# Causal mask of the maxima moved to VectorE, weight parts to GpSimd, and two score units of each half merged

## What is computed

```python
H, D = (NUM_HEADS, HEAD_DIM)                       # 32 heads of 16
qkv = hidden_states @ w_attn + b_attn
scores = jnp.einsum('bqhd,bkhd->bhqk', q, k) * SCALE
bias = slopes[:, None, None] * rel[None, :, :]     # rel = key position - query position
causal = rel <= 0
scores = jnp.where(causal[None, None], scores + bias[None], -jnp.inf)
attn = jax.nn.softmax(scores, axis=-1)
out = jnp.einsum('bhqk,bkhd->bqhd', attn, v).reshape(B, S, HIDDEN)
return out @ w_proj + b_proj
```

## Time and profile before

| what | us |
| --- | --- |
| median of 3 runs (1851.12 to 2012.93) | 1870.08 |
| the profiled execution | 1866.97 |
| its span, first to last instruction | 1865.1 |
| busy in the span: PE / DVE / ACT / POOL | 1744.0 / 1366.6 / 987.7 / 119.7 |

### The profile page before, as it was taken

One profiled execution on the slowest core, in us unless ns is written; L12 is line 12 of the kernel. 1 busy time (PEld: TensorE's weight loads), 2 busy tenths in 40 slices (PEclk: granted clock), 3 DMA queues, 4 the chain that ended last, 5 costly groups with the idle time before them and its releaser, 6 DMA issues. The chain is left out here.

```text
span 1865.1 us, 35240 instructions
## 1 busy us (share of the span) xinstructions
PE 1744.0 (94%) x14412; PEld 904.9 (49%) x14412; DVE 1366.6 (73%) x2495; ACT 987.7 (53%) x1169; POOL 119.7 (6%) x218
## 2 busy tenths in 40 slices
PE   6997999999999999999799998899999999999697
PEld 4553433333333333333347677555555555543486
DVE  3765799999999999996464542588787878762485
ACT  3332277777777777778301111056666666655210
POOL 3323000000000000000010000100000000002000
PEclk9998799999999999999899999999999999975699
DMA  7768304332333333321524246815445444511221
GB/s 212 211 190 213 63 15 87 65 70 53 53 53 56 53 53 53 64 46 58 149 64 135 69 115 208 160 28 107 81 80 89 72 84 77 87 30 56 83 85 68
DMA packets 116865, 167.67 MB, mean 90 GB/s; under 512 B 20828, under 2 KB 58092, under 8 KB 116588
## 3 DMA queue, kind: packets, MB, share of 16 engines
q1 hardware_dynamic: 114880, 160.11, 38.1%
q0 software_dynamic: 1824, 5.31, 1.6%
HBM read 100.34 MB, written 64.50 MB: 88 GB/s over the span
## 5 line engine op out<-in xcount | busy, mean ns | idle before, releaser
L513 DVE TENSOR_REDUCE a_mxp<-a_ps_m 128x1 f32<-128x512 f32 x1024 | 634.2, 683 | 48.3 <-PE a_ps_m L377 44.9
L492 ACT ACTIVATE a_p<-a_ps_s 128x1024 f32<-128x1024 f32 x512 | 522.4, 1025 | 170.6 <-PE a_ps_s L417 160.9
L513 DVE TENSOR_REDUCE b_mxp<-b_ps_m 128x1 f32<-128x512 f32 (+3 forms) x768 | 382.3, 551 | 116.8 <-PE b_ps_m L377 109.6
L492 ACT ACTIVATE b_p<-b_ps_s 128x1024 f32<-128x1024 f32 (+3 forms) x384 | 308.8, 810 | 231.3 <-PE b_ps_s L417 229.0
L377 PE MATMUL a_ps_m<-a_slot_qk 48*128 48x512 f32 x640 | 240.0, 452 | 0.9
L417 PE MATMUL a_ps_s<-a_slot_qk 50*128 50x512 f32 x640 | 233.1, 445 | 1.2
L436 PE MATMUL a_ps_o<-a_p,a_slot_v 128*32 128x256 f32 x2560 | 205.6, 390 | 10.0 <-ACT a_p L492 5.4
L417 PEld LDWEIGHTS a_ps_s<-a_slot_qk 50*128 50x128 f32 x640 | 96.4, 185 | 128.8 <-issue 122.7
L377 PE MATMUL a_ps_m<-slot_qk 48*128 48x512 f32 x384 | 145.7, 469 | 0.4
L417 PE MATMUL a_ps_s<-slot_qk 50*128 50x512 f32 x384 | 140.3, 466 | 2.2 <-DMA slot_qk<-a_cturned 1.6
L436 PE MATMUL a_ps_o<-a_p,slot_memory 128*32 128x256 f32 x1536 | 127.9, 403 | 7.3 <-ACT a_p L492 3.3
(11 more groups left out here) (166 smaller groups left out, 2453.7 us busy)
## 6 DMA issues: line engine op xcount, KB each, us to landing
va_groups<-w_o SPq DMA_DIRECT2D x16, 512.0 KB, 3.7
ka_parts<-pa_parts SPq DMA_DIRECT2D x16, 512.0 KB, 3.8
qa_parts<-pa_parts SPq DMA_DIRECT2D x32, 256.0 KB, 3.7
kb_parts<-slot_memory SPq DMA_DIRECT2D x16, 512.0 KB, 3.5
qb_parts<-slot_memory SPq DMA_DIRECT2D x32, 256.0 KB, 3.5
vb_groups<-w_proj SPq DMA_DIRECT2D x16, 512.0 KB, 3.2
a_slot_qk<-qa_parts SPq DMA_DIRECT2D x60, 128.0 KB, 4.5
a_slot_qk<-ka_parts SPq DMA_DIRECT2D x48, 128.0 KB, 6.9
```

The source lines that it names most:

```text
L492: act.activation(p_sb[:, (2 * u + pair) % NP, :, off:CHUNK], ps_s[:, 2 * pair:2 * pair + 2, off:CHUNK], ACT.Exp, scale=scale).then_inc(exp ...
L513: dve.tensor_reduce(to, from_, AX.X, ALU.max).then_inc(piece_taken, 1)
```

## The change

Three things change, all in attention B (A takes the same code with one block in each unit).

- The 1024 mask matmuls of the maxima go. VectorE adds the mask itself: `tensor_tensor_reduce` reads the piece from PSUM and a bf16 mask from SBUF (0 in all columns but the last 128), writes the sum back in place and the maximum to `mxp`. It takes the place of `tensor_reduce` for the 32 diagonal pieces of each group. The masks of the scores stay on PE.
- The 256-wide and the 128-wide unit of each half become one unit whose scores lie side by side in one bank (columns 256 to 511 and 128 to 255). Its exponential is one instruction of 384 columns for two heads; its values take the 128-wide block as part 0 and the 256-wide one as part 1. A group has 10 units, with 6, 4, 4, 4, 6, 6, 4, 6, 4, 4 pieces.
- The high parts of the two weights are copied by GpSimd, right ahead of each subtraction, at the end of its list. ACT's two copies go.

```diff
-    units = [(qh, kt) for qh in range(2) for kt in range((4 * (qh + 1)) if causal else 8)]
+    def block(qh, kt):
+        off = max(0, P * kt - CHUNK * qh) if causal else 0
+        return kt, off, CHUNK - off, off
+    units = []
+    for qh in range(2):
+        last = (4 * (qh + 1)) if causal else 8
+        for kt in range(last - (2 if causal else 0)):
+            units.append((qh, [block(qh, kt)]))
+        if causal:
+            (_, _, _, at), (kt, off, n, _) = wide, narrow = block(qh, last - 2), block(qh, last - 1)
+            units.append((qh, [wide, (kt, off, n, at - n)]))
...
             for n, (whole, high, low_part) in enumerate(to_split):
+                pool.tensor_copy(high[:, :, :], whole[:, :, :]).then_inc(w_high_ready, 1)
                 pool.wait_ge(w_high_ready, n + 1)
...
-                diagonal = causal and half == qt // 4
-                if diagonal:
-                    add_mask(ps_m[:, bank_of(g, i), keys - P:keys], mask_of_query, row)
-                pe.matmul(ps_m[:, bank_of(g, i), 0:keys], q, k, start=not diagonal, stop=True,
-                          skip_group_check=diagonal).then_inc(piece_ready, 1)
+                pe.matmul(ps_m[:, bank_of(g, i), 0:keys], q, k, start=True, stop=True).then_inc(piece_ready, 1)
...
+                to = ps_s[:, PAIR * pair + e, :]
+                for kt, off, n, at in blocks:
+                    k = slots[j].k[row:row + rows, pair, kt * P:(kt + 1) * P]
+                    q = slots[j].q[row:row + rows, qh, pair, off:off + n]
+                    diagonal = causal and P * kt >= CHUNK * qh
+                    if diagonal:
+                        add_mask(to[:, at:at + P], mask_of_key, row)
+                    mm = pe.matmul(to[:, at:at + n], k, q, start=not diagonal, stop=True, skip_group_check=diagonal)
...
+                if len(blocks) == 1:
+                    kt, off, _, at = blocks[0]
+                    lo, hi = max(off, part * CHUNK // 2), (part + 1) * CHUNK // 2
+                else:
+                    kt, off, n, at = blocks[1 - part]
+                    lo, hi = off, off + n
...
-                if s == NG - 3 and to_split:
-                    act.wait_ge(late_loaded, 16 * len(late))
-                    for whole, high, _ in to_split:
-                        act.activation(high[:, :, :], whole[:, :, :], ACT.Copy).then_inc(w_high_ready, 1)
...
-                dve.tensor_reduce(to, from_, AX.X, ALU.max).then_inc(piece_taken, 1)
+                if causal and half == qt // 4:
+                    if g == 0:
+                        dve.wait_ge(masks_loaded, 16)
+                    dve.tensor_tensor_reduce(from_, from_, mask_of_query[:, CHUNK - keys:], 1.0, LOWEST,
+                                             ALU.add, ALU.max, accum_out=to).then_inc(piece_taken, 1)
+                else:
+                    dve.tensor_reduce(to, from_, AX.X, ALU.max).then_inc(piece_taken, 1)
```

More of the change, by code:

```diff
@@ L155, in attention @@
     PPU = NPC // NU
-    NPH = PPU * sum(qh == 0 for qh, _ in units)
+    NPH = sum(qt < 4 for _, _, qt, _, _ in pieces)
     AHEAD = PPU * (13 if causal else 11)
-    columns = [CHUNK - (max(0, P * kt - CHUNK * qh) if causal else 0) for qh, kt in units]
+    columns = [sum(n for _, _, n, _ in blocks) for _, blocks in units]
     before_unit = [2 * round(NPC * sum(columns[:u]) / sum(columns) / 2) for u in range(NU + 1)]
@@ L214, in attention @@
         if causal:
[L215 to L218, removed]
+            masks = sb("masks", [P, 2 * P + ROW_TILE + CHUNK], BF16)
+            mask_of_key = masks[:, 0:2 * P].rearrange("p (a n) -> p a n", a=2)
+            half_ident = masks[:, 2 * P:2 * P + ROW_TILE]
+            mask_of_query = masks[:, 2 * P + ROW_TILE:]
         ps_s = ctx.enter_context(nc.psum_tensor(f"{tag}_ps_s", [P, 4, CHUNK], F32))
@@ L401, in scores @@
             def scores(s, j, u, pair, e):
-                qh, kt = units[u]
-                off = max(0, P * kt - CHUNK * qh) if causal else 0
-                diagonal = causal and P * kt >= CHUNK * qh
+                qh, blocks = units[u]
                 if u == first_of[qh] and pair == 0 and e == 0:
@@ L422, in values @@
             def values(s, j, u, part):
-                qh, kt = units[u]
-                off = max(0, P * kt - CHUNK * qh) if causal else 0
-                lo, hi = max(off, part * CHUNK // 2), (part + 1) * CHUNK // 2
+                qh, blocks = units[u]
+                if len(blocks) == 1:
[4 more added lines that the diff above has]
+                    lo, hi = off, off + n
                 pe.wait_ge(exp_done, s * NT + (2 * u + 2))
@@ L436, in values @@
                     mm = pe.matmul(ps_o[VW * h:VW * (h + 1), lo:hi], slots[j].v[:, kt, VW * h:VW * (h + 1)],
-                                   p_sb[:, (2 * u + h // 2) % NP, h % 2, lo:hi],
+                                   p_sb[:, (2 * u + h // 2) % NP, h % 2, at + lo - off:at + hi - off],
                                    start=(u == first_of[qh] and part == 0), stop=(u == last_of[qh] and part == 1))
@@ L485, in step @@
             def step(s):
-                for u, (qh, kt) in enumerate(units):
-                    off = max(0, P * kt - CHUNK * qh) if causal else 0
+                for u, (qh, blocks) in enumerate(units):
+                    off = min(at for _, _, _, at in blocks)
                     wait_past(act, pv_done, s * NU + (u - 1))
@@ L1553, in shape_constants @@
     row, column = (np.arange(P) % ROW_TILE)[:, None], np.arange(P)[None, :]
-    masks = [np.where(row + half * ROW_TILE > column, NEG, 0.0) for half in range(2)]
-    masks += [np.where(column > row + half * ROW_TILE, NEG, 0.0) for half in range(2)]
-    masks = np.concatenate(masks + [np.where(row == np.arange(ROW_TILE)[None, :], 1.0, 0.0)], axis=1)
+    masks = [np.where(column > row + half * ROW_TILE, NEG, 0.0) for half in range(2)]
+    masks += [np.where(row == np.arange(ROW_TILE)[None, :], 1.0, 0.0), np.zeros((P, CHUNK - P))]
+    masks += [np.where(column > np.arange(P)[:, None], NEG, 0.0)]
+    masks = np.concatenate(masks, axis=1)
     base = 2 ** (-2 ** (-(np.log2(H) - 3)))
```

## The result

The changed kernel took **2078.31 us** (median of 4 runs, 2056.64 to 2092.36), the kernel before 1866.21 us beside it; the ratio is 1.108, 95% interval 1.093 to 1.124. It is slower by a tenth where I forecast 1846 us. The profiled execution took 2068.66 us, its span is 2066.9 us, and the mean granted clock is 0.821 (before: 0.949).

The account below looks back on a forecast made before the run. No engine was full; PE's list tied B's steady groups, with VectorE nearly the bound in dense stretches and half clock in the last two groups. -31.1 + 8.4 + 1 = -21.7 us from 1866.97 gave 1846 us, range 1826 to 1890.

Parts of the forecast that it names:

- Part 1: Attention B, last two groups: weight copies leave ACT, group 14 gains 19.3 us and group 15 11.8, together -31.1 us.
- Part 2: Attention B, maxima's mask moved to VectorE: steady groups 0.6 us longer, +8.4 us over 14, +1 us ahead of them.
- d: Added time from start to start of a diagonal piece's VectorE reduction: taken as 0.10 us, between 0 and 0.33.
- the estimate of 0.075: Alternative added time per VectorE diagonal piece, from the skill's 75 ns fixed cost; said to lower the sum about 5 us.
- the 1.0 us in my sum: VectorE's masks in a steady group of B: +0.9 us in the burst stretch, +0.1 us in the rest.
- PE's saving: Steady group of B without 64 mask matmuls: 0.4 us less, 0.8 us at most.
- The rival in which VectorE becomes the bound: B's groups limited by VectorE, deciding from 0.21 us added per diagonal piece; 1927 us at 0.33; chance 0.15.
- My sign for it: End-of-half copies in steady groups 33 us or more apart would say that VectorE has become the bound.
- Part 3: Merged units in B's groups with pieces: taken as 0, between -0.4 and +0.4 us a group.
- a changed steady group: B's groups with pieces after the change: 31.45 us instead of 30.85, also taken for group 14.
- The sign that I had named for being wrong: Clock falling in group 14 of B with no copies on ACT; the other was above 0.2 us added per diagonal piece.
- the clock falls anyway: Rival for B's last two groups: clock drops without ACT's copies, only their 3.7 us return, 1873 us; chance 0.15.

Follow-up runs that it names:

- Copies and merge: Changed kernel with the maxima's masks back on TensorE (weight copies on GpSimd and merged units remain): 1960.40 us, 1.051 against the kernel before.

## Why the prediction was wrong

**Part 1, the copies: right.** I forecast -31.1 us; alone they brought 29.3 us (1864.86 to 1835.61). Group 14, with nothing else changed, takes 30.3 us. Group 15 takes 24.0 us, the figure of the forecast, but that agreement is in part luck: the forecast was for merged units, and for these 12 units its sum would give about 25. With merged units only runs with doubled scores kept the full clock there (25.2 to 28.4 us). GpSimd's list in the kernel after (in the run with the copies alone it has the same durations):
```profile
1898.37 1.89 POOL L295 CAST w_proj_high<-w_proj 128x2048 fp32r<-128x2048 f32 x1
1900.34 4.54 POOL L297 TENSOR_TENSOR w_proj_low<-w_proj,w_proj_high 128x2048 fp32r<-128x2048 f32 x1
1904.82 1.89 POOL L295 CAST w_eff_high<-w_eff 128x2048 fp32r<-128x2048 f32 x1
1906.80 4.53 POOL L297 TENSOR_TENSOR w_eff_low<-w_eff,w_eff_high 128x2048 fp32r<-128x2048 f32 x1
```
A copy takes 1.89 us (I had 0 to 4.5) and the chain 13.0 us (18 at most). With the copies alone, the next nearest path was this:
```profile
1691.42 2.50 DVE L1130 TENSOR_TENSOR out_b_o_t<-out_b_o_t,out_b_rzt 128x512 f32<-128x512 f32 x4 [16.14 <-DMA out_b_rzt<-zb_reciprocals]
```
It ends 4.8 us ahead of the last copy at 1698.71; I had given it 3 us.

**Part 2, the price on VectorE: oversized.** Timeline of DVE after, three diagonal pieces, and the groups by shape:
```profile
1429.12 0.73 DVE L525 CUSTOM_DVE_ANT_0 b_ps_m<-b_ps_m,b_masks 128x512 f32<-128x512 f32 x1
1429.77 0.14 DVE L525 DVE_READ_ACCUMULATOR2_ANT b_mxp<- 128x1 f32 x1
1429.77 0.73 DVE L525 CUSTOM_DVE_ANT_0 b_ps_m<-b_ps_m,b_masks 128x512 f32<-128x512 f32 x1
1430.41 0.14 DVE L525 DVE_READ_ACCUMULATOR2_ANT b_mxp<- 128x1 f32 x1
1430.41 0.33 DVE L525 CUSTOM_DVE_ANT_0 b_ps_m<-b_ps_m,b_masks 128x128 f32<-128x128 f32 x1
```
```profile
L525 DVE CUSTOM_DVE_ANT_0 b_ps_m<-b_ps_m,b_masks 128x512 f32<-128x512 f32 x128 | 87.3, 711 | 32.8 <-PE b_ps_m L387 32.4
L525 DVE DVE_READ_ACCUMULATOR2_ANT b_mxp<- 128x1 f32 x512 | 72.4, 141 | 0.0
```
There are two rows for a piece, as the Trainium skill says (VectorE: DVE Perf Modes, "Two Vector instructions with no wait between them"). But the second starts with the next piece's first, and from start to start a 512-wide piece takes 0.64 to 0.65 us. In the run with VectorE's mask, the filler and 12 units, a pair of them took 1.25 us from start to start and a pair of plain reductions 1.21: d = 0.02 to 0.05 us, where I took 0.10. The fixed cost in the Trainium skill (Vector Engine (DVE) Microarchitecture Reference, "Measured stream behaviour on trn2") would have given the estimate of 0.075. By my own terms that would have lowered the sum by about 4 us, not 5. At full clock VectorE's masks cost 0.29 us a group there (31.14 against 30.85) and 0.40 in the merged form (30.73 with the filler against 30.33), against the 1.0 us in my sum ahead of PE's saving. The rival in which VectorE becomes the bound is out: at full clock, with the filler, DVE is busy 26.1 of 30.6 us. My sign for it, a period of 33 us or more, could not tell it from a fallen clock.

**PE's saving: within its bound in time, and blind to the clock.** The second half's masks gone brought 0.33 us a group at full clock (30.40 with half the filler against 30.73 with all), and the first half's, added once more, cost 0.34. All of them gone never ran at full clock; my estimate from these two is 0.67 us, where I had 0.4 and 0.8 at most.

**Part 3, the merge: -0.5 us a group** at full clock (30.33 against 30.85, and 30.80 with the copies alone), just outside my 0 +- 0.4.

**The step that failed** is the one on which these sums stood: "Group 14 then has nothing ahead of it that differs from the fourteen before it. I take its time as that of a changed steady group, 31.45 us", and 14 x 0.6 = +8.4 us for the steady groups. Both price a changed group at clock 1.00, because the earlier trace rows show 1.00 through fourteen groups. A group at half clock takes 48.2 us, 17 us more, and no term and no rival had that for groups 0 to 13: +199 us there and 10 in group 0, and 22.6 us of part 1's 31.1 lost again, since groups 14 and 15 took 46.2 and 31.9 us in place of 31.45 and 24.0. The sign that I had named for being wrong, the clock falling in group 14 with no copies on ACT, came true, and it fell in the groups ahead as well. The rival "the clock falls anyway" looked at the last two groups only. It has the right words, "PE gets lighter by the masks", and prices them nowhere; the same rows show 0.55 after a disturbance of 3.7 us, which could have told me that 1.00 is a state with an edge (their 0.95 for the stretch ahead says less: it is the end of an earlier low spell, with 0.57 from 1178 to 1186 us), and that an edit that takes work from PE needs a price on the clock, not on columns alone.

**Shown, and still open.** Shown: the loss is PE at half clock, and more than one edit brings it about. Taking PE's mask matmuls away does so with VectorE untouched; in the 12 units VectorE's mask does so with PE's list kept in full; the merge does so alone, in every second group. In the changed kernel, putting the matmuls back as useless work regains the clock in all groups with pieces, with VectorE's masks in place. Of the two halves of that filler, the first, around the start of a group, holds the clock in half of the groups, the second in none. Open: what exactly is weighed. "Copies and merge" falls, and the changed kernel with filler, whose PE list is the same but for which maker of a mask is real, holds, at a period 0.4 us longer; in the 12 units the longer period of VectorE's mask goes with the fall instead. Doubling the scores at the end of a group held the clock with PE's masks and did not without. The two ends shown of one kernel agree and part. I can give no rule that sorts all these kernels.

## What to carry to other kernels

Where a loop runs at 2.4 GHz with every engine partly waiting, work of TensorE that looks like pure cost may be what holds its clock: before taking it away, price the loop at half clock as a rival (here 48.2 against 30.3 us a group) and make the edits one at a time. If the time gets worse by more than any instruction can explain, look at the granted clock of each group first, and try the removed matmuls as overwritten filler, at the place where the clock falls. Here, on top of PE's masks, 32 small ones a group cost 0.34 us of it and gave back 17 to 18 in each group that had fallen; in the 12 units with VectorE's mask the whole filler held it only through group 3.

## What was unexpected of the hardware

- The granted clock fell to 0.50 with hardly a gap of TensorE in the profile: in the 31 us up to the fall of "copies and merge" shown above, the only wait was 0.2 us, and the kernel that holds its clock has the same one. The Trainium skill (TensorE: Matmul & The Clock Gate, "HAM oscillation — how this bites in real kernels") ties such falls to idle gaps of PE in waits for DMA; the fall shown here has no such wait ahead of it. Its next section, "A second HAM failure mode: psum-queue depth-cycling", puts a clock that swings between its two levels down to frequent short idle spells of PE between groups of matmuls. That is nearer, but no run here shows such spells: PE's listed times contain waiting inside the engine and could hide them.
- In the kernel after, the clock once down came back mostly 27 or 44 us later (twice 140), and fell again 3 to 5 us into a group: groups 1 to 14 take 41 us or 46 to 48 us, none between.
- The operation with a second result shows as two rows of 711 and 141 ns, yet adds only 0.02 to 0.05 us to a reduction of 684 ns from start to start.
- GpSimd copies 128x2048 fp32 into fp32r in 1.89 us, as fast as ScalarE did (1.90 us).
